# Attention scores made a second time with keys on partitions, in place of turned tiles

## The reference, cut to what matters

```
Q, K, V = (x @ W + b) split in 16 heads of 8          # 4 batches, 512 queries, 512 keys
val  = sin(pq)cos(pk) + sin(pk)cos(pz) + sin(pz)cos(pq) - threshold
mask = sigmoid(val / (temperature + 1e-6))            # one 512 x 512 mask for each head
scores = Q @ K.T / sqrt(8) + 0.3 * log(mask + 1e-6)
out = softmax(scores) @ V @ Wo + bo
```

## Time and profile before

| | us |
|---|---|
| median of 3 runs | 2267.85 (2265.78 to 2277.2) |
| profiled execution, its own time | 2271.8 |
| its span, first to last instruction | 2270.0 |
| steps of the attention, first score to last result copied | 498.7 to 911.7 |

### The profile page before, as it was taken

How to read it: one execution, slowest core, us unless ns; L and a number is a source line. 1 busy time by engine, 2 the same in 40 slices (tenths; PEclk the granted TensorE clock), 3 DMA queues, 4 the chain that set the end, 5 groups by cost and what they waited for, 6 DMA issues and landing times.

```text
span 2270.0 us, 42540 instructions
## 1 busy us (share of the span) xinstructions
PE 1844.4 (81%) x14557; PEld 1161.8 (51%) x14620; DVE 1530.6 (67%) x2433; ACT 1226.5 (54%) x2826; POOL 1073.0 (47%) x865
## 2 busy tenths in 40 slices
PE   5899999759888888479999974698679889984796
PEld 2556555325555555256566542487234645532585
DVE  6778887367998898567778846487354455326585
ACT  3676666457999897347766645243432322334242
POOL 3656666246777678256656632433133133005233
PEclk7999999867999899679999996699789999996797
DMA  6000000120001001000000003200400000000202
GB/s 230 2 2 2 2 2 2 36 70 19 20 22 26 19 21 47 7 1 2 2 2 1 2 1 121 76 22 30 141 0 0 1 0 0 1 0 29 65 22 71
DMA packets 46014, 63.40 MB, mean 28 GB/s; under 512 B 9184, under 2 KB 35552, under 8 KB 45120
## 3 DMA queue, kind: packets, MB, share of 16 engines
q1 hardware_dynamic: 41312, 51.96, 7.3%
q0 software_dynamic: 4544, 9.35, 1.3%
HBM read 45.26 MB, written 21.18 MB: 29 GB/s over the span
## 4 chain that ended last, share of the span: by engine, by line
PE 35%; DVE 9%; issue 6%; ACT 6%; POOL 1%; DMA 1%; DVEq 0%; SPq 0%; ACTq 0%; POOLq 0%
PE PS L1791 3%; PE PS L1773 2%; PE PS L470 2%; PE PS L1775 2%; PE PS L1774 2%; DVE arena L801 1%; PE PS L1781 1%; PE PS L2416 1%; PE PS L2387 1%; ACT arena L664 1%; PE PS L2433 1%; PE PS L2429 1%; PE PS L2363 1%; PE PS L2437 1%; PE PS L2364 1%
## 5 line engine op out<-in xcount | busy, mean ns | idle before, releaser
L1565 POOL TENSOR_TENSOR arena<-arena 128x1024 f32<-128x1024 f32 x128 | 299.7, 2362 | 128.2 <-ACT arena L1499 128.2
L664 ACT ACTIVATE arena<-PS,arena 128x128 f32<-128x128 f32 x512 | 180.2, 370 | 118.7 <-DVE arena L828 118.4
L1004 POOL TENSOR_TENSOR arena<-arena 128x512 f32<-128x512 f32 x128 | 132.4, 1040 | 223.9 <-DVE arena L835 222.1
L340 PE MATMUL PS<-arena_r 128*128 128x512 f32 x216 | 118.9, 551 | 94.1 <-DVE arena_r L1986 43.2
L1473 PE MATMUL PS<-con,arena 128*128 128x128 f32 x1024 | 155.2, 296 | 49.4 <-DVE arena L1549 47.0
L801 DVE SCALAR_TENSOR_TENSOR arena<-PS,fcol,big 128x512 f32<-128x512 f32 x256 | 177.3, 741 | 15.8 <-PE PS L342 8.5
L1473 PEld LDWEIGHTS PS<-con,arena 128*128 128x128 f32 x1024 | 117.3, 148 | 121.5 <-issue 94.8
L1549 DVE COPY arena<-PS 128x512 f32<-128x512 f32 x256 | 165.4, 684 | 20.5 <-PE PS L1473 20.3
L1499 ACT ACTIVATE arena<-PS,arena 128x512 f32<-128x512 f32 x256 | 154.9, 688 | 40.2 <-DVE arena L1530 38.6
L1510 ACT ACTIVATE arena<-arena 128x512 f32<-128x512 f32 x256 | 162.5, 636 | 23.5 <-DVE arena L1537 17.4
L2097 POOL DMA_INDIRECT expert_y<-arena x78 | 74.5, 955 | 200.4 <-DVE arena L2056 151.2
(11 more groups left out here) (374 smaller groups left out, 4685.0 us busy)
## 6 DMA issues: line engine op xcount, KB each, us to landing
big<-in_gu SPq DMA_DIRECT2D x16, 512.0 KB, 8.1
sorted_x<-in_slots SPq DMA_DIRECT2D x2, 2515.5 KB, 15.6
arena<-sorted_x SPq DMA_DIRECT2D x6, 774.0 KB, 7.4
big<-in_dn SPq DMA_DIRECT2D x16, 256.0 KB, 8.9
arena<-expert_y SPq DMA_DIRECT2D x16, 256.0 KB, 3.3
arena<-q_split SPq DMA_DIRECT2D x96, 32.0 KB
arena<-k_split SPq DMA_DIRECT2D x96, 32.0 KB
heads_out<-arena SPq DMA_DIRECT2D x128, 16.0 KB
```

What stands on the lines that cost most here:

```text
L340: pe.matmul(bank, w_hi, hi, start=first, stop=False)
L664: act.activation(pr[:, u % 2, t, :], PS[:, u % 2, t * P:(t + 1) * P], ACT.Exp, bias=nmax[:, u % 2, t:t + 1], accum_out=psum_[:, u % 2, t:t ...
L1004: g.tensor_tensor(pn[:, u % 2, :, :], pr[:, u % 2, :, :], pinv[:, u % 2, :].unsqueeze(2).broadcast_to([P, TPB, P]), ALU.mult).then_inc(s(" ...
L1565: g.tensor_tensor(a, a, mk[:, hp, 2 * half:2 * half + 2, :], ALU.mult).then_inc(s("a_masked"), 1)
```

## The change

Nothing is turned any more. PE makes each step's scores twice. The first time is as before (`score`), but only to take the maxima from them; it is done in two halves through banks 0 and 1. DVE takes the maxima in two instructions of 1024 columns, splits each negated maximum into two bfloat16 parts (`max_parts`: a copy `hi` and a difference `lo`, each 128 x 4, SBUF to SBUF), PE turns them into two rows (`turn_max`, four matmuls of 2 columns x 128, bank 7), and DVE copies the two rows behind the head's 48 rows, as rows 64 and 65 of `q_st` (`max_row`). Rows 48 to 63 are zero and rows 64 and 65 of `k_st` are one (six memsets on POOL ahead of the loop). The second time (`shifted`) the product runs over these 66 rows with keys on partitions, so that the maximum is already subtracted and the result is turned (banks 2 to 5). ACT takes its exponential without a bias, in two instructions of 1024 columns, into `pp`, which `values` reads directly. The mask's argument is made turned (its two factors change places), and ACT's five functions run over pairs of tiles, 1024 columns at a time, in a buffer `mz` in the place of `ppT`; the last one writes `mk`. `stepping` calls one `body` on each engine. SP loads heads behind counts of `a_exp` and factors behind counts of `mask_clamped`.

```diff
+        def stepping(body, i_range, lead):
+            for st in range(-lead, 0):
+                body(0, st)
+            with i_range(0, PASSES - 1) as i:
+                for st in range(STEPS):
+                    body(i, st)
...
-                for t in range(TPB):
-                    pe.wait_ge(s("a_exp"), ...)
-                    pe.matmul(PS[:, t, :], q_st[hp][0:KS, b, t * P:(t + 1) * P], k_st[hp][0:KS, b, :], ...)
+            def score(i, st, half):
+                    pe.wait_ge(s("a_nmax"), START + at(i, MAX_OPS * STEPS, MAX_OPS * st + (1 if half else 2 - MAX_OPS)))
+                for k in range(PAIR):
+                    t = PAIR * half + k
+                    mm = pe.matmul(PS[:, k, :], q_st[hp][0:KS, b, t * P:(t + 1) * P], k_st[hp][0:KS, b, :], start=True, stop=True)
...
-                    for kt in range(TPB):
-                        tr = pe.transpose(PS[:, 4 + t % 2, kt * P:(kt + 1) * P], pp[:, st % 2, t, kt * P:(kt + 1) * P], ident)
+            def turn_max(i, st, clamped):
+                pe.wait_ge(s("a_nmax"), START + at(i, MAX_OPS * STEPS, MAX_OPS * (st + 1)))
+                pe.wait_ge(s("mask_clamped"), START + clamped)
+                for t in range(TPB):
+                    mm = pe.matmul(PS[ROW_MAX:KX, TURN_BANK, t * P:(t + 1) * P], a_parts[:, st % 2, t, :], ident_b[:], start=True, stop=True)
+            def shifted(i, st, half):
+                if half == 0:
+                    pe.wait_ge(s("max_rows"), START + at(i, STEPS, st + 1))
+                pe.wait_ge(s("a_exp"), ...)
+                for k in range(PAIR):
+                    kt = PAIR * half + k
+                    mm = pe.matmul(PS[:, 2 + kt, :], k_st[hp][0:KX, b, kt * P:(kt + 1) * P], q_st[hp][0:KX, b, :], start=True, stop=True)
...
+            def body(i, st):                       # PE
+                    score(*later(i, st + 2), 1)
+                    shifted(*later(i, st + 1), 0)
+                    argument(*later(i, st + STEPS), TURN_BANK)
+                    score(*later(i, st + 3), 0)
+                    shifted(*later(i, st + 1), 1)
+                    turn_max(*later(i, st + 2), ...)
+                    values(i, st)
...
+            def body(i, st):                       # ACT
+                    exponential(*later(i, st + 1), 0)
+                    mask(*later(i, q), masks[0])
+                    exponential(*later(i, st + 1), 1)
+                    mask(*later(i, q), *masks[1:])
+                    copied(i, st)
...
-                v.tensor_reduce(a_nmax[:, st % 2, :], PS[:, 0:TPB, :], AX.X, ALU.max, negate=True)
+            def maxima(i, st, half):
+                v.tensor_reduce(a_nmax[:, st % 2, PAIR * half:PAIR * half + PAIR], PS[:, 0:PAIR, :], AX.X, ALU.max, negate=True)
+            def max_parts(i, st):
+                v.tensor_copy(hi, m).then_inc(s("a_nmax"), 1)
+                v.tensor_tensor(lo, m, hi, ALU.subtract).then_inc(s("a_nmax"), 1)
+            def max_row(i, st):
+                v.tensor_copy(q_st[hp][ROW_MAX:KX, b, :], PS[ROW_MAX:KX, TURN_BANK, :]).then_inc(s("max_rows"), 1)
...
-                    v.tensor_copy(ppT[:, :, t * P:(t + 1) * P],
-                                  PS[:, 4 + t % 2, :].rearrange("p (a b) -> p a b", a=TPB)).then_inc(s("ppT_ready"), 1)
+            def body(i, st):                       # DVE
+                    maxima(*later(i, st + 2), 1)
+                    max_parts(*later(i, st + 2))
+                    clamp(*later(i, st + STEPS), TURN_BANK)
+                    maxima(*later(i, st + 3), 0)
+                    max_row(*later(i, st + 2))
```

More of the change, by code:

```diff
@@ L1393, in attn_sync, with one @@
                 load_mask_factors(0, hp)
+            sp.wait_ge(s("parts0_stored"), START + 192)
+            sp.wait_ge(s("parts1_stored"), START + 192)
+            sp.wait_ge(s("head_pads"), START + 6)
+            for hp in range(HEADS_PER_PASS):
                 load_head(0, hp)
[L1396 to L1405, removed]
+            sp.wait_ge(s("mask_clamped"), START + TPB)
+            load_mask_factors(1, 0)
+            def one(i, left):
+                if left >= 1:
+                    sp.wait_ge(s("mask_clamped"), START + at(i, STEPS, 2 * TPB))
+                    load_mask_factors(i + 1, 1)
+                    sp.wait_ge(s("a_exp"), START + at(i, 2 * STEPS, 2 * B))
+                    load_head(i + 1, 0)
+                store(i, 0)
+                if left >= 2:
+                    sp.wait_ge(s("mask_clamped"), START + at(i, STEPS, 3 * TPB))
+                    load_mask_factors(i + 2, 0)
+                if left >= 1:
+                    sp.wait_ge(s("a_exp"), START + at(i, 2 * STEPS, 4 * B))
+                    load_head(i + 1, 1)
+                store(i, 1)
+            with sp.Fori(0, PASSES - 2) as i:
+                one(i, 2)
+            one(PASSES - 2, 1)
             done = (PASSES - 1) * HEADS_PER_PASS * HD
@@ L1415, in attn_sync @@
             sp.dma_start(o_all[done:], o_dram[0, done:]).then_inc(s("o_loaded"), 16)
[L1417 to L1443, removed]
         def attn_pe(pe):
@@ L1447, in attn_pe, with argument @@
             pe.wait_ge(s("a_values"), START + B + 2)
-            def scored(i, st):
+            def score(i, st, half):
                 hp, b = st // B, st % B
-                if b == 0:
+                if b == 0 and half == 0:
                     pe.wait_ge(s(f"head{hp}_loaded"), START + at(i, 12 * 16, 12 * 16))
-                for t in range(TPB):
[L1454 to L1458, removed]
+                if half or not (type(i) is int and i == 0 and st == 0):
+                    pe.wait_ge(s("a_nmax"), START + at(i, MAX_OPS * STEPS, MAX_OPS * st + (1 if half else 2 - MAX_OPS)))
+                for k in range(PAIR):
+                    t = PAIR * half + k
+                    mm = pe.matmul(PS[:, k, :], q_st[hp][0:KS, b, t * P:(t + 1) * P], k_st[hp][0:KS, b, :], start=True, stop=True)
+                mm.then_inc(s("a_scores"), 1)
+            def argument(i, q, bank):
                 hp, tile = q // TPB, q % TPB
@@ L1486, in values @@
                 mm.then_inc(s("a_pv"), 1)
-            stepping(pe, scored, quarter, values, turned)
-        def attn_act(act):
[L1491 to L1512, removed]
@@ new lines, in body @@
+            def body(i, st):
+                if exists(i, st + 2):
+                    score(*later(i, st + 2), 1)
+                if st >= -1 and exists(i, st + 1):
+                    shifted(*later(i, st + 1), 0)
+                if exists(i, st + STEPS):
+                    if st >= -1:
+                        pe.wait_ge(s("max_rows"), START + at(i, STEPS, st + 2))
+                    argument(*later(i, st + STEPS), TURN_BANK)
+                if exists(i, st + 3):
+                    score(*later(i, st + 3), 0)
+                if st >= -1 and exists(i, st + 1):
+                    shifted(*later(i, st + 1), 1)
+                if exists(i, st + 2):
+                    turn_max(*later(i, st + 2), at(i, STEPS, st + STEPS + 1) if exists(i, st + STEPS) else TILES)
+                if st >= 0:
+                    values(i, st)
@@ new lines, in attn_pe, with exponential, mask, copied @@
+            for q in range(STEPS - 2):
+                argument(0, q, 2 + q)
+            pe.wait_ge(s("mask_clamped"), START + STEPS - 2)
+            score(0, 0, 0)
+            stepping(body, pe.Fori, 2)
+        def attn_act(act):
+            act.wait_ge(s("consts"), START + 10)
+            def exponential(i, st, half):
+                act.wait_ge(s("a_shifted"), START + at(i, 2 * STEPS, 2 * st + half + 1))
+                if half == 0 and not (type(i) is int and i == 0 and st < 2):
+                    act.wait_ge(s("a_pv"), START + at(i, STEPS, st - 1))
+                act.activation(pp[:, st % 2, PAIR * half:PAIR * half + PAIR, :], PS[:, 2 + PAIR * half:2 + PAIR * half + PAIR, :],
+                               ACT.Exp).then_inc(s("a_exp"), 1)
+            def mask(i, q, *steps):
+                hp, pair = q // TPB, q % TPB // PAIR
+                z = mz[:, pair, :, :]
+                done = MASK_OPS * q // PAIR
+                for k in steps:
+                    func, bias, scale = ((ACT.Exp, 0.0, 1.0), (ACT.Ln, 1.0, 1.0), (ACT.Exp, 0.0, -1.0),
+                                         (ACT.Ln, c_1e6, 1.0), (ACT.Exp, 0.0, 0.3))[k]
+                    if k == 0:
+                        act.wait_ge(s("mask_clamped"), START + at(i, STEPS, q + PAIR))
+                    else:
+                        act.wait_ge(s("mask_stage"), START + at(i, MASK_OPS * STEPS // PAIR, done + k))
+                    if k == MASK_OPS - 1 and not (type(i) is int and i == 0):
+                        act.wait_ge(s("a_masked"), START + at(i, 2 * STEPS, 2 * B * (hp - 1)))
+                    dst = mk[:, hp, PAIR * pair:PAIR * pair + PAIR, :] if k == MASK_OPS - 1 else z
+                    act.activation(dst, z, func, bias=bias, scale=scale).then_inc(s("mask_stage"), 1)
```

(22 more changed lines are left out.)

132 lines of the change are left out of this document (80 added, 52 removed).

## The result

The changed kernel is slower by 1.3%: 2300.0 us (median of 4 runs, 2294.3 to 2312.0) against 2272.1 for the kernel before beside it, a ratio of 1.0131 with a 95% interval from 1.0079 to 1.0183. The forecast was 2360 with a range of 2280 to 2405. The sign and the range held; the size, +28 where +92 was forecast, did not.

A forecast was written before the change was run, and what follows sets the result against it. It took ACT and DVE to bound the loop at 2.4 GHz (6.0 us a step), PE at 1.2 GHz (9.5). Lead 14.1, 56 steps of 8.0 and 43 for the last eight made 505 against 413.0 us: 2360, range 2280 to 2405.

The forecast's parts named there:

- PE's step at 1.2 GHz: PE in the attention loop: without turned tiles, with second scores, turn and cuts, 8.0 us a step, from 9.52.
- DVE's prices: DVE in each step: maxima 1.22 us each, clamp 0.744, row copy 0.683, hi and lo 0.21 each; 4.3 us in all.
- nothing left in it raises the clock: TensorE clock in the loop: stays at 1.2 GHz without turned tiles, so PE sets 8.0 us a step; chance 0.70.
- the first rival: Loop clock rises now and then; half the steps at 5.5 us, mean 6.75, 21 us more, 2289; chance 0.12.
- new wait: PE before turn_max: DVE needs 2.7 us while PE has 4.85 of other work, so no stall unless hi and lo are held up.
- the second rival: DVE late at 1.2 GHz: hi and lo held by POOL's multiplications, 10.5 us a step, 140 us more, about 2500; chance 0.05.
- the third rival: Loop mostly at 2.4 GHz: step between 4.7 and 6.7 us, taken as 5.5; 47 us less, 2221; chance 0.13.

The follow-up runs named there:

- rows kernel: Changed kernel with the second scores over 128 rows instead of 66, the added rows of q zero; 2295.5 us, ratio to before 1.0101.
- both: Changed kernel with second scores over 128 rows, maxima not split into hi and lo, and head's values copied by ACT; 2171.6 us, ratio to before 0.9550.
- rows with split: Changed kernel with second scores over 128 rows and maxima not split into hi and lo; head's values still copied by DVE; 2222.0 us, ratio 0.9807.
- split with head: Changed kernel with maxima written as one bfloat16 row (no hi, lo) and head's values copied by ACT; 2237.2 us, ratio to before 0.9846.
- rows with head: Changed kernel with second scores over 128 rows and head's values copied by ACT; hi and lo stay on DVE; 2276.5 us, ratio to before 1.0032.
- head alone: Changed kernel with only the copy of a head's values moved from DVE to ACT; 2263.3 us, ratio to before 0.9976.

## Why the prediction was right in sign and wrong in size

**Right: PE's step at 1.2 GHz.** 8.0 forecast, 8.08 measured, with PE busy 98% of such a stretch and each term within 0.15 us of its price. So were DVE's prices, except for the held copies.

**Wrong: the clock.** The step that failed is the forecast "that nothing left in it raises the clock. Then PE sets the step at 8.0 us." It read a cause out of three coincidences: all rises of before stood behind turned tiles, but turned tiles ran in each step, also in those in which nothing rose. After, the clock rises behind scores and values with no turned tile in the loop, and its mean is 0.64 (502 to 912), not 0.50. The mean step became 7.01 for 8.0, so 56 x 0.99 = 55 us of the 92 did not come: 2364 - 55 = 2309, against 2312.0 profiled. That is the first rival, "the clock rises now and then", with its mean of 6.75 and 2289; it had a chance of 0.12. The range held because it was drawn wide enough to take that rival in.

**The sign held by luck.** The 55 us are the net of two errors that stand against each other. Without held copies the 56 steps take 5.73 us each, not 8.0; the held copies bring them to 7.01, by PE's waits and by a lower clock (0.65 for 0.77 in the window). The copies of results of that kernel, first and 57th:

```profile
515.73 0.26 ACT L1562 ACTIVATE arena<-PS 128x128 f32<-128x128 f32 x1
836.80 0.26 ACT L1562 ACTIVATE arena<-PS 128x128 f32<-128x128 f32 x1
```

So with nothing held the changed kernel is faster than the kernel before, against the forecast (ratio 0.9846, and 0.9976 with the head copies alone moved). What makes it slower are held copies, for which the sum had no term.

**Missed: the copy of the head's values.** The prediction's new wait was right in kind ("no stall, unless `hi` and `lo` are held up") and looked at the wrong instruction first. The earlier trace rows already showed the head copy at 1.68 us beside a multiplication; it stays in the changed kernel, behind the second maxima on DVE, and no term was made for it. At 8.08 us a step it is what starts the hold-up, and moving it to ACT is worth 37 us, more than the whole difference of 28. As for `hi` and `lo`, the second rival's argument against them (POOL is idle 3.3 of 8.0 us) mostly held at 1.2 GHz: all twelve `hi` of over 1.5 us from 520 to 912 follow a held head copy. It fails at 2.4 GHz, where POOL has no pause: the rows kernel shows both held in one step.

**Where the gain went.** The changed kernel has less to do on ACT and DVE than the one before (1163.1 us for 1226.5, 1503.5 for 1530.6 over the span), and with the clock up a step of 4.7 us was there to be had, the floor that the third rival gave (it took 5.5); 2171.6 shows it. The kernel after has neither of the two things that it takes. With 65 or 66 rows in the second scores the clock is 0.65 to 0.77 in all four kernels, whichever copies are on DVE, and the copies on DVE can stop PE where they are held beside a multiplication on POOL. Rows alone gave 4.5 us (its interval and the one of the kernel after overlap), no held copies 63, both 128: the rows are worth 66 us, but only where nothing is held.

The Trainium skill, "SBUF — State Buffer", section "SBUF: two separate sides", tells of a pair of ports that VectorE and GpSimd share and that one of them holds for a whole instruction, while the other is blocked. The traces agree in that the held copies shown above end as a multiplication does, within 0.1 us; that one copy waited through more than two of them (5.72 us beside multiplications of 2.35) goes beyond what the section states. That the ports are what holds them was not measured in itself.

The Trainium skill, "TensorE: Matmul & The Clock Gate", section "Part 1: The HAM clock gate", explains the level of the clock by how busy TensorE has been. The runs agree where a long wait of PE precedes a fall (2.58 us in rows, 5.36 in rows with split). With busy time as the profile counts it they disagree for split with head: there PE waits for nothing, is busy 174.00 of 174.00 us, and has 0.77, while with 128 rows, busy 172.42, it has 0.98. The profile models the ends of matmuls, so such shares are generous. An estimate by steps, with 4.04 us of work at 2.4 GHz (half of 8.08), gives about 4.1 us of each 4.6 us step with 128 rows and 5.2 of 5.6 with 65, so PE was not busier with 128 rows by this measure either.

**Open.** That 128 rows keep the clock up where 65 don't is shown (0.98 and 0.77); no other number of rows was tried. Why eight matmuls of 128 rows a step do not do it, and what brings on the rises in the kernel after, is not settled. A kernel that keeps turned tiles in the loop beside the second scores was not tried, so that they held the clock up in the kernel before is not shown either.

## What to carry to other kernels

Before you remove matmuls that look like mere rearrangement, ask what the others do to the clock by themselves, and don't take what stood before each rise for its cause if it also ran where nothing rose. A tiny copy from SBUF to SBUF on DVE beside a busy POOL was priced here by POOL's instructions, not by its size; let the instruction that reads PSUM write the final type, or give the copy to ACT. Look for both, held copies and matmuls that leave rows empty, since removing one may show little of its worth until the other is gone too.

## What was not expected of the hardware

A cast of 128 x 4 numbers took from 0.17 us to 2.29, and a copy of 128 x 128 from 0.21 to 5.72, by what POOL did. DVE's instructions that read PSUM and write SBUF were not held: the maxima took 1.22 us in the kernel after and all nine variants, also with a bfloat16 result, and the casts of rows 0.69. Second scores over 128 rows took as long as over 66 (1.04 us for two at 1.2 GHz). ACT's copy of the head's values took 0.30 us beside the same multiplications. And a higher clock can go with a longer time: rows with head has 0.76 where head alone has 0.69, and takes 13 us more.
